# Root of the deviations moved to VectorE, diagonals to ScalarE, shifted stream summed from the bank, in the local transformers of an eight-layer kernel

## The reference, cut to what matters

```python
x = x + attn_layer(shift_tokens(x), Wqkv, q_scale, k_scale, Wo)   # 16 heads of 64, windows of 32
x = x + ffn_layer(shift_tokens(x), g, bln, W1, b1, W2, b2)
def shift_tokens(t):        # the second half of the channels comes from the token before
    a, s = split(t, 2); return concatenate([a, pad_one_token(s)[:-1]])
def ffn_layer(x, ...):
    mu = x.mean(-1); var = ((x - mu) ** 2).mean(-1)
    xn = (x - mu) / sqrt(var + 1e-05) * g + bln
    a, gate = split(xn @ W1 + b1, 2)
    return a * gelu(gate) @ W2 + b2
```

## Time and profile before

| | |
|---|---|
| median of 3 runs | 4838.06 us |
| profiled execution, its own time | 4835.69 us |
| its span, first to last instruction | 4833.7 us |
| mean granted TensorE clock | 0.930 |
| busy: PE, DVE, ACT, POOL | 4105.6, 3395.1, 3389.8, 3646.1 us |
| first local stage | 555 to 2349 us of the span |
| second local stage | 2613 to 4407 us |

### The profile page before, as it was taken

How to read it: one execution, slowest core, us unless ns; L and a number is a source line. 1 busy time by engine, 2 the same in 40 slices (tenths; PEclk the granted TensorE clock), 3 DMA queues, 4 the chain that set the end, 5 groups by cost and what they waited for, 6 DMA issues and landing times. The chain is left out here.

```text
span 4833.7 us, 128817 instructions
## 1 busy us (share of the span) xinstructions
PE 4105.6 (85%) x47211; PEld 2659.9 (55%) x47211; DVE 3395.1 (70%) x5981; ACT 3389.8 (70%) x10612; POOL 3646.1 (75%) x5558
## 2 busy tenths in 40 slices
PE   5888799999999999999504999999999999995675
PEld 2222266666666666666302666666666666663353
DVE  6999767767767667666496767667667667664657
ACT  4666488888888888888202888888888888884121
POOL 2777689889888888888365988888888888882323
PEclk7999899999999999999756999999999999997787
DMA  1000101101011010010001111110110100100000
GB/s 25 0 0 0 47 23 40 31 24 46 23 41 30 22 50 22 22 37 22 3 0 47 26 37 30 28 40 25 41 30 22 50 22 22 37 22 3 5 3 9
DMA packets 69295, 121.54 MB, mean 25 GB/s; under 512 B 24872, under 2 KB 46052, under 8 KB 67172
## 3 DMA queue, kind: packets, MB, share of 16 engines
q1 hardware_dynamic: 68708, 113.70, 9.0%
HBM read 35.56 MB, written 1.05 MB: 8 GB/s over the span
## 5 line engine op out<-in xcount | busy, mean ns | idle before, releaser
L1233 ACT ACTIVATE local_pr<-local_tb,local_nmax 128x96 f32<-128x96 f32 x3072 | 1022.9, 372 | 158.1 <-DVE local_nmax L1363 154.7
L932 POOL TENSOR_TENSOR local_qk<-local_qk,local_rb 128x512 f32<-128x512 f32 x768 | 970.5, 1273 | 112.8 <-DVE local_rb L1351 110.5
L1056 PE MATMUL local_pj<-local_wqkv,local_xs 128*128 128x512 f32 x1536 | 836.5, 638 | 23.9 <-DVE local_rb L1351 11.9
L938 POOL TENSOR_TENSOR local_qk<-local_qk,local_rinv 128x512 f32<-128x512 f32 x768 | 788.9, 1044 | 0.3
L968 POOL TENSOR_TENSOR local_pr<-local_pr,local_rsum 128x384 f32<-128x384 f32 x768 | 626.7, 827 | 203.1 <-DVE local_rsum L1369 203.1
L1233 ACT ACTIVATION_READ_ACCUMULATOR local_pr<-local_tb,local_nmax 128x1 f32 x3072 | 733.5, 239 | 0.0
L1348 DVE TENSOR_TENSOR local_qk<-local_pj,local_rope 128x512 f32<-128x512 f32 x768 | 522.7, 681 | 172.0 <-ACT local_sq L1216 115.4
L1351 DVE TENSOR_TENSOR local_rb<-local_pj,local_rope 128x512 f32<-128x512 f32 x768 | 523.9, 682 | 112.9 <-POOL local_qk L932 112.9
L1363 DVE TENSOR_REDUCE local_nmax<-local_tb 128x4 f32<-128x384 f32 x768 | 416.6, 554 | 247.0 <-PE local_tb L1083 243.9
L1216 ACT ACTIVATE local_sq<-local_pj 128x512 f32<-128x512 f32 x768 | 471.4, 628 | 162.4 <-PE local_pj L1056 157.3
L1358 DVE TENSOR_REDUCE local_ss<-local_sq 128x8 f32<-128x512 f32 x768 | 502.8, 675 | 26.6 <-ACT local_sq L1216 26.4
(11 more groups left out here) (382 smaller groups left out, 8168.3 us busy)
## 6 DMA issues: line engine op xcount, KB each, us to landing
local_v<-local_v SPq DMA_DIRECT2D x288, 256.0 KB, 3.8
local_wqkv<-L_ffn_Wqkv_dram SPq DMA_DIRECT2D x12, 1536.0 KB, 8.4
local_wo<-L_ffn_Wo_dram SPq DMA_DIRECT2D x12, 512.0 KB, 5.3
local_w<-L_ffn_W_dram SPq DMA_DIRECT2D x12, 341.0 KB, 2.9
mamba_parts<-mamba_in_low SPq DMA_DIRECT2D x12, 128.0 KB, 2.3
local_w<-L_ffn_W_dram SPq DMA_DIRECT2D x12, 128.0 KB
y_dram<-store_xtok SPq DMA_DIRECT2D x4, 256.0 KB, 2.5
local_oT<-rope_dram SPq DMA_DIRECT2D x2, 256.0 KB, 2.9
```

What stands on the lines that cost most here:

```text
L932: nc.gpsimd.tensor_tensor(qk[:, u, :], qk[:, u, :], rb[:, u % 2, :], ALU.add).then_inc(s["summed"], 1)
L938: nc.gpsimd.tensor_tensor(heads8(qk[:, u, :]), heads8(qk[:, u, :]), r, ALU.mult).then_inc(s["scaled"], 1)
L1056: nc.tensor.matmul(bank[:, :], xs[:, par, u // 4 * P:(u // 4 + 1) * P], wqkv[:, dep % 2, u % 4 * BANK:(u % 4 + 1) * BANK], start=True, sto ...
L1233: ins = nc.scalar.activation(pr[:, (NU * c + k) % PR_RING, i, WIN:WIN + KW], scores[:, i * KW:(i + 1) * KW], ACT.Exp, bias=nmax[:, k, i:i ...
```

## The change

`POOL_STEPS` stays for the roots of q and k; the root of the deviations gets `STD_STEPS = 10` steps on VectorE, on a tile `newton` [128, 2, 2, 7] in which neighbours are laid out so that one reduce by multiplication or addition does each operation (three per Newton step, not four). The diagonals are made on ScalarE. `shift2` is gone: `residual1` sums z and the bank three times, twice into `xs2` (64 partitions each, the second shifted by a token) and once into a new tile `z1`; `residual2` reads z from `z1`. `affine` writes to the second half of `fb`, and the wait for `up` goes to `bias_xn`.

```diff
             def centre(e, par, _):
                 pe.wait_ge(s["xs2_ready"], 2 * e + 2)
+                pe.wait_ge(s["z1_ready"], e + 1)
...
+            def spread_std(e, par, _):
+                act.wait_ge(s["std_steps"], STD_STEPS * e + STD_STEPS)
+                need(act, s["spread"], e)
+                for t in range(2):
+                    ins = nc.scalar.activation(diag[:, t, :], net.ident[:, :], ACT.Copy, scale=newton[:, 1, t, 1:2])
+                ins.then_inc(s["diag_ready"], 1)
...
                 act.wait_ge(s["xn0_ready"], e + 1)
-                nc.scalar.activation(xn[:, :], xn[:, :], ACT.Identity, bias=cols[:, e // B, 8:9]).then_inc(s["xn_ready"], 1)
+                need(act, s["up_ready"], 3 * e)
+                nc.scalar.activation(xn[:, :], fb[:, L:2 * L], ACT.Identity, bias=cols[:, e // B, 8:9]).then_inc(s["xn_ready"], 1)
...
             def residual1(e, par, _):
+                h = C // 2
                 dve.wait_ge(s["wo_ready"], e + 1)
-                nc.vector.tensor_tensor(z[:, e % B, :], z[:, e % B, :], fb[:, 0:L], ALU.add).then_inc(s["z1_ready"], 1)
+                need(dve, s["centred"], e)
+                for own, to, count in ((slice(0, h), 0, L), (slice(h, C), 1, L - 1)):
+                    nc.vector.tensor_tensor(xs2[own, to:to + count], z[own, e % B, 0:count], fb[own, 0:count], ALU.add).then_inc(s["xs2_ready"], 1)
+                need(dve, s["z_ready"], B + e - 1)
+                nc.vector.tensor_tensor(z1[:, e % 2, :], z[:, e % B, :], fb[:, 0:L], ALU.add).then_inc(s["z1_ready"], 1)
...
-                need(dve, s["std_steps"], POOL_STEPS * e)
-                nc.vector.tensor_scalar(var[:, :], fb[:, L:L + 2], LN_EPS, None, ALU.add).then_inc(s["var_in"], 1)
+                need(dve, s["diag_ready"], e)
+                nc.vector.tensor_scalar(var[:, :], fb[:, L:L + 2], LN_EPS, None, ALU.add)
+                nc.vector.tensor_scalar(newton[:, :, :, 3], view(fb[:, L:L + 2], [[0, 2], [1, 2]]), LN_EPS, -0.5,
+                                        ALU.add, ALU.mult).then_inc(s["var_in"], 1)
+
+            def std(e, par, step):
+                i, part = divmod(step - 1, 3)
+                old, new = newton[:, i % 2, :, :], newton[:, (i + 1) % 2, :, 1:3]
+                if step == 0:
+                    dve.wait_ge(s["var_in"], e + 1)
+                    ins = nc.vector.tensor_scalar(newton[:, 0, :, 1:3].bitcast(U32), view(var[:, :], [[1, 2], [0, 2]]).bitcast(U32), -0.5, SEED,
+                                                  ALU.mult, ALU.add)
+                else:
+                    dve.wait_ge(s["std_steps"], STD_STEPS * e + step)
+                    if part == 0:
+                        ins = nc.vector.tensor_reduce(old[:, :, 5], old[:, :, 1:4], AX.X, ALU.mult)
+                    elif part == 1:
+                        ins = nc.vector.tensor_reduce(old[:, :, 0], old[:, :, 5:7], AX.X, ALU.add)
+                    else:
+                        ins = nc.vector.tensor_reduce(new, view(old[:, 0, 0:2], [[7, 2], [0, 2], [1, 2]]), AX.X, ALU.mult)
+                ins.then_inc(s["std_steps"], 1)
...
-                need(dve, s["up_ready"], 3 * e)
-                nc.vector.scalar_tensor_tensor(xn[:, :], fb[:, 0:L], cols[:, e // B, 7:8], cen[:, :], ALU.mult, ALU.mult).then_inc(s["xn0_ready"], 1)
+                nc.vector.scalar_tensor_tensor(fb[:, L:2 * L], fb[:, 0:L], cols[:, e // B, 7:8], cen[:, :], ALU.mult, ALU.mult).then_inc(s["xn0_ready"], 1)
...
                 dve.wait_ge(s["down_ready"], f + 1)
+                dve.wait_ge(s["z1_ready"], f + 1)
-                nc.vector.scalar_tensor_tensor(z[:, f % B, :], fb[:, 0:L], cols[:, f // B, 6:7], z[:, f % B, :],
+                nc.vector.scalar_tensor_tensor(z[:, f % B, :], fb[:, 0:L], cols[:, f // B, 6:7], z1[:, f % 2, :],
```

More of the change, by code:

```diff
@@ L1170, in iteration @@
             def iteration(run):
+                run(up, 5, 0)
+                run(project, 2, 5)
+                run(weigh, 4, 2)
+                run(turn_probs, 4, 3)
+                run(turn_qk, 3, 3)
+                run(project, 2, 6)
+                run(up, 5, 1)
+                run(project, 2, 7)
+                run(score, 3, 0)
+                run(score, 3, 1)
+                run(weigh, 4, 3)
+                run(up, 5, 2)
+                run(project_v, 3, 2)
+                run(project_v, 3, 3)
@@ L1171, in iteration @@
+                run(down, 5, 0)
+                run(score, 3, 2)
+                run(out_project, 4, 0)
+                run(project_v, 2, 0)
+                run(out_project, 4, 1)
+                run(turn_probs, 3, 0)
+                run(score, 3, 3)
+                run(centre, 4, 0)
+                run(project_v, 2, 1)
+                run(variance, 4, 0)
+                run(project, 1, 0)
+                run(turn_qk, 2, 0)
                 run(weigh, 3, 0)
-                run(project_v, 2, 3)
@@ new lines, in iteration @@
+                run(square2, 5, 0)
+                run(exps, 4, 6)
+                run(copy_v, 3, 1)
+                run(square, 2, 0)
+                run(exps, 4, 7)
+                run(copy_qk, 3, 0)
+                run(copy_qk, 3, 1)
+                run(square, 2, 1)
+                run(spread_std, 5, 0)
+                run(copy_qk, 3, 2)
+                run(copy_qk, 3, 3)
+                run(copy_probs, 4, 2)
+                run(square, 2, 2)
+                run(copy_probs, 4, 3)
@@ L1323, in _ @@
+                run(copy_qk, 3, 7)
+                run(gelu, 5, 2)
+                run(square, 2, 7)
+                run(exps, 3, 0)
+                run(copy_v, 3, 2)
+                run(exps, 3, 1)
+                run(exps, 3, 2)
+                run(exps, 3, 3)
+                run(copy_v, 3, 3)
+                run(exps, 3, 4)
+                run(exps, 3, 5)
+                run(copy_probs, 3, 0)
+                run(copy_probs, 3, 1)
             pipeline(act, iteration)
@@ new lines, in iteration @@
+                run(rotate, 2, 6)
+                run(sum_squares, 2, 6)
+                run(gate, 5, 0)
+                run(sum_squares, 2, 7)
+                run(maxima, 3, 0)
+                run(rotate, 2, 7)
+                run(gate, 5, 1)
+                run(maxima, 3, 1)
+                run(gate, 5, 2)
+                run(maxima, 3, 2)
+                run(maxima, 3, 3)
+                run(shift_in, 1, 0)
+                run(residual2, 5, 0)
+                run(recip, 3, 0)
+                run(maxima, 3, 4)
```

302 lines of the change are left out of this document (108 added, 194 removed).

## The result

The changed kernel takes 4617.81 us, the median of 4 runs (4611.48 to 4622.09), against 4838.35 for the kernel before beside it: a ratio of 0.9542, 95% interval 0.9526 to 0.9559. It is faster by 4.6%; the forecast was 4683 with a range of 4648 to 4800, so it gained 65 us more than the forecast and 30 more than the range allowed.

The account below looks back on a forecast made before the run. TensorE was taken as the bound, its idle time as waits on POOL. Per stage 93.3 us from 44 periods plus 1, less 14 and 3, gave 77.4; two stages 155, so 4835.7 became 4681, as median 4683; range 4648 to 4800.

Parts of the forecast that it names:

- the wait for the diagonals: TensorE before spread: 1.20 us a period, put down to the root of the variances on POOL, expected to go.
- The wait for the scaled unit: TensorE waiting for the first scaled q/k unit, behind the root in POOL's queue: 0.39 us a period, expected to go.
- Rival A: TensorE runs without gaps in the local stages: 4683 us, 4650 to 4725 with periods from 33.8 to 34.4; chance 0.64.
- ScalarE's queue: Two diagonals at 0.61 us, reached at 28.3 in the placement, 0.8 us before spread; ScalarE the next late thing, not VectorE.
- an iteration issues the same matmuls, so TensorE's floor stays 33.94 us: TensorE's work per local-stage iteration, taken as unchanged by the new order; with 0.05 charged, a period of 34.0 us.
- The moves behind Wo: SP's queue: v lands late behind Wo, weigh waits 2.0 us five times a stage; 10 + 4 us with low clock.
- Filling and draining: Start and end of each stage: a longer sequence costs 3 us more (0 to 9); the first period gives 1.
- The lock: Root's step 0, a tensor_scalar on VectorE beside POOL: 0.2 to 1.4 us, taken as 0.2; at 1.4 project 3 waits 0.5.
- B: A handoff late by some 0.6 us in each iteration, low clock back at its present share: 4789 us; chance 0.22.
- C: VectorE's reduces cost 0.46 us a step, spread and project 3 wait, 1.5 us in all: slower, 4870 us; chance 0.10.
- The margins: Handoffs in the new queue orders, walked over the bank pairs and projection banks: all hold, by 0.3 us or more.
- The sums of residual 1: Three VectorE sums from the bank, starting 0.34 us after one another, end at 20.9; centre at 21.2, free by 0.3.

Follow-up runs that it names:

- root_only: The kernel before with only the ten-step root moved from POOL to VectorE, diagonals still on POOL, old orders: 4648.68 us, ratio 0.9602.
- root_on_pool: move_v_first with the root back on POOL, 13 steps behind norm_p 4, diagonals still on ScalarE: 4687.55 us, ratio 0.9651.
- split_pairs: move_v_first with three pairs of TensorE steps of the same kind taken apart by other steps, same work: 4638.84 us, ratio 0.9583.
- two_inputs: move_v_first with the root's nine reduces replaced by scalar_tensor_tensor and tensor_tensor on 128x2, still on VectorE: 4727.12 us, ratio 0.9736.
- together_retimed: move_v_first with project 1 directly behind project 0, copy_v 1 ahead of exps 6, and three ScalarE and two VectorE steps exchanged: 4801.99 us, ratio 0.9930.
- root_longer: move_v_first with seven Newton iterations in place of three, 22 root steps on VectorE instead of 10: 4851.65 us, ratio 1.0019.
- The three attempts at a better order: move_v_first with project 1 behind turn_probs 1 (4727.41 us), or directly behind project 0 (4573.13 us), or the latter with ScalarE and VectorE steps exchanged (4801.99 us).
- move_v_first: The changed kernel with move_v ahead of next_wo in SP's queue, nothing else: 4568.24 us, ratio 0.9436.
- shift_on_act: move_v_first with the shifted stream made by two ScalarE copies from z1 after one VectorE sum: 4621.67 us, ratio 0.9516.

## Why the prediction was right and wrong

**Right.** TensorE bounds the stage, and the wait for the diagonals came from the root's place on POOL: root_only took the root away, and the wait vanished with it. The wait for the scaled unit, which the prediction put down to the same queue, stayed in root_only and is gone in root_on_pool; it went with the rest of the change. Rival A's picture holds: no matmul waits in a usual period, the clock is 1.00 in it, and the only gaps are the ten before weigh 0. The reduces were taken at 0.21 us and stand 0.195 apart, the diagonals at 0.61 and take 0.68. ScalarE's queue, not VectorE's chain, decides when the diagonals are made, by 0.17 us: the last reduce ends at 1199.88, and ScalarE, without a pause before it, reaches them at 1200.05. They end at 1200.73, 0.8 us before spread, as forecast.

**The step that failed** is "an iteration issues the same matmuls, so TensorE's floor stays 33.94 us". It issues the same matmuls, and its floor is 33.24. The distance of two starts is not a property of the first step alone: it depends on its neighbours and on whether one of them waits. The prediction took each step's distance from the earlier trace rows, where two waits stood in each period, and carried them over as constants. In us per period, summed from the distances in the timelines without the waits:

| | before | root_only | after | split_pairs |
|---|---|---|---|---|
| q/k projections | 7.45 | 7.29 | 7.86 | 8.01 |
| v projections | 3.89 | 3.88 | 3.49 | 3.49 |
| spread | 0.71 | 0.69 | 0.44 | 0.55 |
| turns (both kinds) | 4.99 | 4.99 | 4.68 | 5.00 |
| the other steps | 16.90 | 16.90 | 16.77 | 17.03 |
| all | 33.94 | 33.75 | 33.24 | 34.08 |

Of the 0.70, 0.16 is the tail of the projection before spread, which root_only shows by itself; some 0.25 is spread's own, in front of the second wait (0.69 in root_only, 0.44 behind a projection and before one). The remaining 0.26 to 0.29 go to the new order. It is a balance of gains and losses: three pairs of turns stand together where one did (0.3 less), four v projections have fewer turns and scores beside them (0.4 less), two scores stand together (0.1 less), and the q/k projections have more of them beside them and lose 0.6 from root_only to after. That an order alone can do this is shown (split_pairs, 0.84 for three exchanges); each exchange was not run by itself.

**The terms.** Per stage the forecast was 77.4 less, and it was 109.2. The period gave 44 x (34.0 - 33.24) = 33.4 more. The moves behind Wo gave 22.6 - 14 = 8.6 less: mechanism and number of times were as forecast, the size was not. The gaps are 3.0 us and not 2.0, since Wo and the moves took 8.0 us from the first issue (1154.48) to weigh's start and not 7.0, and the lower clock comes behind each. Filling and draining were put at a loss of 2 us (3 for the longer chain, 1 gained) and gained 5: 109.2 - 44 x 2.88 + 22.6. So 33.4 - 8.6 + 7 = 31.8 more per stage, 64 in two: 4681 becomes 4617, and the profiled execution took 4620. The moves and the filling were each off by 7 to 9 us, and that they nearly cancel is luck.

**The lock.** Step 0 was priced at 0.2 us, with 1.4 as the other end; it is 0.89 on average, nearly in the middle. It begins beside a POOL instruction that ends at 1196.98, and ends at 1197.01. It cost nothing, because ScalarE was the later of the two before spread; the 0.5 us of wait that the prediction put on a step of 1.4 did not appear at 0.9. What matters is that nine of ten steps are of the kind that is not held: two_inputs, where they are of the kind that is held, gave back 159 of the 270 us.

**The clock in the rivals.** B and C add the low clock at its present share to any late handoff. The runs do not show that: two_inputs waits 0.67 and 0.42 us in each period, together_retimed 0.86 and 1.09, and both have a granted clock of 1.00 and no long period, while the kernel before (1.20 and 0.39) and root_longer (1.29 and 0.46) have long ones. B's 1.2 us a period was 0.6 of wait and 0.6 of clock. In root_on_pool, with waits of 0.43 and 0.22, the period is 1.13 over 33.24, and what is not wait is in the distances of the steps, at a clock of 1.00.

**The margins.** The sums of residual 1 start 0.45 us after one another (1192.68 and 1193.13), not 0.34; the last ends at 1193.55 and centre starts at 1193.72, free by 0.17 and not by 0.3. That all handoffs hold was right, that they hold by 0.3 us or more was not. The three attempts at a better order show how near the edge it is: each moves a few steps and finds a new wait.

**What each part is worth.** The root off POOL some 190 us (root_only). The rest, 80 us from there to move_v_first, is the POOL wait of 0.39, what the steps around it pay, and the order; within it the sum from the bank is worth 53 (shift_on_act). In the kernel after, 50 of this are lost by the order of two lines in SP's queue. The parts lean on one another, and do not add up.

## What to carry to other kernels

When a queue of matmuls has no wait left, its length is still not a constant: a wait costs its idle time plus the tail of the step before it and something in the steps behind it (0.53 us on 1.75 of idle time in root_longer), and steps cost more where neighbours of another tile shape stand. Before counting a bound as fixed, take the distance of starts of each kind of step in each neighbourhood in which it occurs. A rare step (a weight load once in eight iterations) belongs behind the step that the critical engine waits for, also in a queue that seems idle. And a chain of tiny steps on VectorE beside a busy GpSimd is best written in operations that ran beside it unheld, here reduces over neighbours.

## What was not expected of the hardware

- A matmul step's cost depends on its neighbours: spread 0.44 us between projections, 0.55 behind a turn, 0.69 before a wait, 0.55 or 0.71 behind one; a turn 0.54 before a turn, 0.64 alone; two projections together 1.89, apart 2.09. Five more changes of shape cost 0.84 us.
- A tensor_scalar on 128x4 (0.17 us at the least) took 0.94 beside GpSimd, a tensor_tensor on 128x2 took 0.80 and a scalar_tensor_tensor on 128x2 1.26: each ended when GpSimd's instruction did. None of the 432 reduces of the first stage took over 0.17.
- A wait of 0.39 us in each period left the granted clock at 1.00 (root_only), and so did two of 0.86 and 1.09 (together_retimed, 1.95 us idle in 35.86). With one of 1.20 and one of 0.39 (the kernel before, 1.59 in 35.52) it fell to 0.95 in 16 of 44 periods, and one of 2.9 us was followed by matmuls at about the lower level.
